# The end of a delta-rule layer as a stream of tiles, with the next layer's norm and router inside it

## The reference

```
# gated delta rule, 4 heads, keys of 64, values of 128
h = rmsnorm(layernorm(x))                      # x: the residual so far
q, k, v = l2norm(conv_silu(h @ Wq)), l2norm(conv_silu(h @ Wk)), conv_silu(h @ Wv)
o = gated_delta_rule(q, k, v, g, beta)          # scan over the 64 tokens of a sequence
o = rmsnorm(o) * o_norm_w * silu(h @ Wg)
y = x + o @ Wo                                  # here x is the block's own input (a normed x)
x = x + gelu(layernorm(y) @ W2 + b2) + y
# mixture of experts, top 1 of 8
logits = x_n @ Wr + br                          # x_n = layernorm(x) without weights
idx, gate = argmax(logits), softmax(logits)[idx]
x = x + gate * (gelu(x_n @ W1[idx] + b1[idx]) @ W2[idx] + b2[idx])
```

## Time and profile before

| | us |
|---|---|
| median of 3 runs | 843.79 |
| lowest, highest | 839.43, 844.43 |
| the profiled execution | 846.05 |
| its span | 844.3 |
| TensorE busy in the span | 684.7 (81%) |
| VectorE, ScalarE, GpSimd busy | 421.2, 328.4, 144.2 |

### The profile page before, as it was taken

One profiled execution on the slowest core, in us unless ns is written; L12 is line 12 of the kernel. 1 busy time (PEld: TensorE's weight loads), 2 busy tenths in 40 slices (PEclk: granted clock), 3 DMA queues, 4 the chain that ended last, 5 costly groups with the idle time before them and its releaser, 6 DMA issues. The chain is left out here.

```text
span 844.3 us, 18960 instructions
## 1 busy us (share of the span) xinstructions
PE 684.7 (81%) x7638; PEld 525.9 (62%) x7638; DVE 421.2 (50%) x907; ACT 328.4 (39%) x881; POOL 144.2 (17%) x213
## 2 busy tenths in 40 slices
PE   3778887789899999995787689989986764278996
PEld 2556665565456666663665546579985643178995
DVE  5436787764545445514587275836657344011111
ACT  1235444443445544442577363331224141132332
POOL 1011112201100000003334232091000211211121
PEclk9879998999999999995889699989998965598999
DMA  6920000001900000004000000000000009791110
GB/s 174 357 65 2 2 2 1 1 1 34 230 2 2 1 2 1 2 1 127 2 2 3 1 0 2 2 2 2 0 2 2 0 4 318 274 368 39 46 51 23
DMA packets 33161, 45.30 MB, mean 54 GB/s; under 512 B 7998, under 2 KB 26175, under 8 KB 32960
## 3 DMA queue, kind: packets, MB, share of 16 engines
q1 hardware_dynamic: 28672, 33.31, 12.3%
q0 software_dynamic: 2256, 7.37, 2.7%
q10 hardware_dynamic: 2160, 3.60, 1.6%
HBM read 36.91 MB, written 7.89 MB: 53 GB/s over the span
## 5 line engine op out<-in xcount | busy, mean ns | idle before, releaser
L393 ACT ACTIVATE a_pr<-a_bank,a_nms 128x160 f32<-128x160 f32 x128 | 49.1, 391 | 59.4 <-DVE a_nms L723 57.0
L859 PE MATMUL a_bank<-ident,a_pr 128*80 128x128 f32 x256 | 41.5, 289 | 25.7 <-DVE a_pt L699 23.2
L2101 ACT ACTIVATE f_hb<-f_bank,cols 128x128 f32<-128x128 f32 x96 | 35.2, 367 | 63.1 <-PE f_bank L2219 58.2
L859 PEld LDWEIGHTS a_bank<-ident,a_pr 128*80 128x80 f32 x256 | 26.1, 124 | 46.3 <-ACT a_pr L393 31.8
L2219 PE MATMUL f_bank<-f_xts,f_w 128*128 x384 | 51.6, 293 | 0.8 <-DVE f_xts L2171 0.8
L2219 PEld LDWEIGHTS f_bank<-f_xts,f_w 128*128 128x128 f32 x384 | 50.2, 208 | 1.7 <-issue 1.2
L629 DVE TENSOR_REDUCE a_negmx<-a_bank 128x2 f32<-128x320 f32 x64 | 30.4, 475 | 33.6 <-PE a_bank L851 33.6
L699 DVE COPY a_pt<-a_bank 80x512 f32<-80x512 f32 x60 | 40.9, 682 | 10.5 <-PE a_bank L859 9.8
L2229 PE MATMUL f_bank<-f_w,f_hb 128*128 128x256 f32 x192 | 44.0, 383 | 0.0
L2229 PEld LDWEIGHTS f_bank<-f_w,f_hb 128*128 128x128 f32 x192 | 36.2, 194 | 4.5
L358 POOL TENSOR_TENSOR a_spr<-a_linv,a_hm 128x128 f32<-128x128 f32 x32 | 12.1, 400 | 148.9 <-DVE a_linv L678 136.3
(11 more groups left out here) (361 smaller groups left out, 1607.2 us busy)
## 6 DMA issues: line engine op xcount, KB each, us to landing
f_w<-in_f_w SPq DMA_DIRECT2D x16, 1024.0 KB, 9.8
slots<-a_zero POOLq DMA_DIRECT2D x1, 4112.0 KB, 18.7
f_xs<-slots ACTq DMA_DIRECT2D x13, 257.0 KB, 2.7
a_ct<-in_ctxt SPq DMA_DIRECT2D x15, 160.0 KB, 5.1
rows<-in_rows SPq DMA_DIRECT2D x1, 2120.0 KB, 10.1
x<-in_x SPq DMA_DIRECT2D x2, 512.0 KB, 5.1
b_wq<-in_b_wq SPq DMA_DIRECT2D x1, 1024.0 KB, 6.2
b_wk<-in_b_wk SPq DMA_DIRECT2D x1, 1024.0 KB, 8.3
```

The lines of the kernel that those rows point to most:

```text
L393: i = act.activation(pr[:, p, j, k, :], s_bank[j][:, k * KW:(k + 1) * KW], ACT.Exp, bias=nms[:, p, j, k:k + 1], accum_out=rsum[:, p, 2 * j ...
L859: m = pe.transpose(dst[0:HK, (2 * k + a) * P:(2 * k + a + 1) * P], pr[:, p, j, k, a * HK:(a + 1) * HK], c.ident[:, :])
L2101: act.activation(hb[:, m, :], bank[m % 4][:, 0:P], ACT.Gelu, bias=c.col("f_b1", e * FC + m)).then_inc(z["act"], 1)
```

## The change

- The value buffer becomes `c.v0`, a buffer of the whole kernel; two buffers of the first stage are laid into it. `qkv` is split into `qk` and `vv = c.v0`.
- The value transposes move from behind the inversion to the place ahead of it; ScalarE copies them out of PSUM and GpSimd multiplies by `beta`. When all are transposed, SyncE loads the first expert's weights into `c.v0`.
- Behind the inversion the steps over eight tiles become one loop over `NT + 2` steps, in which each engine's queue holds the work of up to three tiles. In it, tile by tile, are the second layer norm, the GELU in two groups of four tiles, and the next stage's norm, transposes and logits in two groups.
- Every root in it is an exponential of -0.5 times a logarithm, and the table set that has both is loaded explicitly (`preload_act_table_set`).
- `stage_f` starts at the maximum of the logits. ScalarE copies the normed tiles into the rows to be scattered. Small constants come with `stage_d`'s loads. Experts 1 to 7 are loaded without the wait for the scatters.

The diff, cut to its core (`ln_vector`, `ln_scalar`, `xt_tensor` and `xt_scalar` are removed whole):

```diff
 @@ stage_d, SyncE
-            sp.wait_ge(z["weights"], 144)
+            sp.wait_ge(z["weights"], 224)
 @@ stage_e, SyncE
+            sp_.wait_ge(z["vt"], NT)
+            sp_.dma_start(vv[:, 0:2, :], c.d["f_w1"][0, :, :].rearrange("(k p) n -> p k n", p=P)).then_inc(z["expert0"], 16)
+            sp_.dma_start(vv[:, 2:4, :].rearrange("p a (m n) -> p (a m) n", n=D), c.d["f_w2"][0, :, :].rearrange("(k p) n -> p k n", p=P)
+                          ).then_inc(z["expert0"], 16)
 @@ stage_e, GpSimd, behind the gate product
+            for t in range(NT):
+                pool.wait_ge(z["vtc"], t + 1)
+                pool.tensor_tensor(bv[:, t, :, :], bv[:, t, :, :], beta[:, t, :].unsqueeze(2).to_broadcast([P, HG, VD]), ALU.mult
+                                   ).then_inc(z["bv"], 1)
 @@ stage_e, ScalarE
             act.wait_ge(z["ssq"], 1)
+            act.preload_act_table_set("natural_log_exp_and_others")
             inverse_lengths(0, bank[0][:, 0:32].rearrange("p (t h) -> p t h", h=HG))
+            for t in range(NT):
+                act.wait_ge(z["vt"], t + 1)
+                act.activation(bv[:, t, :, :].rearrange("p h n -> p (h n)"), bank[t], ACT.Copy).then_inc(z["vtc"], 1)
...
+            for t in range(NT + 2):
+                if t < NT:
+                    act.wait_ge(z["dl"], t + 1)
+                    act.activation(de[:, t, :, :].rearrange("p h n -> p (h n)"), bank[0], ACT.Copy).then_inc(z["de"], 1)
+                if t > 1:
...
+                    for k in range(KC):
+                        a = act.activation(xt2[:, u_ % 2, k, :], bank[5][:, k * P:(k + 1) * P], ACT.Identity,
+                                           scale=c.col("e_g2", k), bias=c.col("e_b2", k))
+                if 0 < t <= NT:
+                    act.wait_ge(z["ogt"], t)
+                    act.activation(de[:, t - 1, :, :].rearrange("p h n -> p (h n)"), bank[3], ACT.Copy).then_inc(z["ogs"], 1)
+                if t < NT:
+                    act.wait_ge(z["o"], t + 1)
+                    act.activation(bv[:, t, :, :].rearrange("p h n -> p (h n)"), bank[1 + t % 2], ACT.Square).then_inc(z["osq"], 1)
+                    act.wait_ge(z["oss2"], t + 1)
+                    act.activation(olog[:, head], oss2[:, head], ACT.Ln, scale=1.0 / VD, bias=eps[:, 0:1]).then_inc(z["olog"], 1)
+                    act.wait_ge(z["olog"], t + 1)
+                    act.activation(orr[:, head], olog[:, head], ACT.Exp, scale=-0.5).then_inc(z["orr"], 1)
+                if 0 < t <= NT:
...                    (logarithm and exponential of tile t - 1's variance: lrs, rs2)
+                if t in (5, 9):
...                    (GELU of four tiles)
+                    act.preload_act_table_set("natural_log_exp_and_others")
...                    (t in (6, 9): roots of the next norm; t in (7, 9): two copies of the router's transposes)
 @@ stage_e, VectorE
+            for t in range(NT + 2):
+                if t < NT:
+                    dve.wait_ge(z["osq"], t + 1)
+                    dve.reduce_sum(oss[:, head], bv[:, t, :, :], AXX).then_inc(z["oss"], 1)
+                    dve.wait_ge(z["oss"], t + 1)
+                    dve.tensor_tensor(oss2[:, head], oss[:, head], rq2[:, t, :], ALU.mult).then_inc(z["oss2"], 1)
+                if t > 1:
+                    dve.wait_ge(z["f2"], t - 1)
+                    dve.tensor_tensor(hb[:, t - 2, :], bank[6][:, 0:D], c.row("e_w2b"), ALU.add).then_inc(z["b2"], 1)
+                if t < NT:
+                    dve.wait_ge(z["orr"], t + 1)
+                    dve.tensor_tensor(ors[:, head], orr[:, head], rq[:, t, :], ALU.mult).then_inc(z["ors"], 1)
+                    dve.wait_ge(z["ors"], t + 1)
+                    for hh in range(HG):
+                        a = dve.scalar_tensor_tensor(bv[:, t, hh, :], bank[1 + t % 2][:, hh * VD:(hh + 1) * VD],
+                                                     ors[:, HG * t + hh:HG * t + hh + 1], gw[:, t, hh, :], ALU.mult, ALU.mult)
+                    a.then_inc(z["og"], 1)
+                if 0 < t <= NT:
+                    v = t - 1
+                    dve.wait_ge(z["enc"], v + 1)
+                    dve.tensor_tensor(x1[:, v, :], xl[:, v, :], bank[4][:, 0:D], ALU.add).then_inc(z["x1"], 1)
...                    (bn_stats, bn_aggr, wait for rs2, then the normed tile:)
+                    dve.tensor_scalar(xn2[:, v % 2, :], x1[:, v, :], w.mv[:, v, 0:1], rs2[:, v:v + 1], ALU.subtract, ALU.mult
+                                      ).then_inc(z["xn2"], 1)
+                if t in (5, 9):
...                    (last add to c.x and statistics of four tiles; t in (6, 9): their normed tiles, c.xn)
 @@ stage_e, TensorE, ahead of the inversion
-            pe.wait_ge(z["gate"], NT)
-            pe.wait_ge(z["lss"], 2)
+            for t in range(NT):
+                pe.wait_ge(z["gate"], t + 1)
+                if t == 0:
+                    pe.wait_ge(z["lss"], 2)
+                for hh in range(HG):
+                    a = pe.transpose(bank[t][:, hh * P:(hh + 1) * P], vv[:, hh, t * P:(t + 1) * P], c.ident[:, :])
+                a.then_inc(z["vt"], 1)
+            pe.wait_ge(z["vtc"], 4)
 @@ stage_e, TensorE, behind the inversion
+            for t in range(NT + 2):
+                if t < NT:
+                    pe.wait_ge(z["bv"], t + 1)
+                    if t:
+                        pe.wait_ge(z["de"], t)
+                    apply(bank[0], xbd, bv, t, z["dl"])
+                if t > 1:
+                    u_ = t - 2
+                    pe.wait_ge(z["xn2"], u_ + 1)
+                    if u_:
+                        pe.wait_ge(z["xt2"], u_)
+                    for k in range(KC):
+                        a = pe.transpose(bank[5][:, k * P:(k + 1) * P], xn2[:, u_ % 2, k * P:(k + 1) * P], c.ident[:, :])
+                    a.then_inc(z["xt2p"], 1)
+                if 0 < t <= NT:
+                    pe.wait_ge(z["og"], t)
...                    (four transposes of tile t - 1's output into bank 3)
+                if t < NT:
+                    pe.wait_ge(z["de"], t + 1)
...
+                    apply(bank[1 + t % 2], abd, de, t, z["o"])
+                if t > 1:
+                    pe.wait_ge(z["xt2"], u_ + 1)
...                    (second weight product of tile t - 2 into bank 6)
+                if 0 < t <= NT:
+                    pe.wait_ge(z["ogs"], t)
...                    (output projection of tile t - 1 into bank 4)
+                if t == 7:
+                    routes(0)
+            routes(1)
 @@ stage_f, SyncE
-            for e in range(E):
-                if e > 1:
+            for e in range(1, E):
+                if e > 2:
                     sp.wait_ge(s_w[e - 2], 32)
-                if e == 3:
-                    sp.wait_ge(z["scattered"], 16 * NT)
 @@ stage_f, ScalarE
-            ln_scalar(act, s, c.w)
-            xt_scalar(act, s, bank, xt)
-            act.wait_ge(z["sh"], NT)
+            for t in range(NT):
+                act.activation(xb[:, t, 0:D], c.xn[:, t, :], ACT.Copy).then_inc(z["ncopy"], 1)
+            act.wait_ge(z["sh"], 1)
 @@ stage_f, VectorE
-            for t in range(NT):
-                dve.tensor_scalar(sh[:, t, :], lg[:, t, :], mx[:, t:t + 1], None, ALU.subtract).then_inc(z["sh"], 1)
+            dve.tensor_tensor(sh[:, :, :], lg[:, :, :], mx[:, :].unsqueeze(2).to_broadcast([P, NT, E]), ALU.subtract
+                              ).then_inc(z["sh"], 1)
```

336 lines of the change are left out of this document (149 added, 187 removed).

## The result

The changed kernel takes 858.43 us (median of 4 runs, 856.49 to 859.38), against 841.84 us for the kernel before in the same session (839.43 to 844.43): ratio 1.0194, 95% interval 1.0151 to 1.0237. It is slower by some 2%, and the forecast of 855.9 us was 2.5 us short. The profiled execution has a span of 857.6 us, 13.3 more than the one before.

The account below looks back on a forecast made before the run. TensorE, busy 81%, was taken as bound, its gaps deciding. First product 627.6, stream 85.7, clock 5 and stage change 1.25 gave 719.5; the last stage's 136.9 made 856.4, less 0.5: 855.9 us, range 832 to 872.

Parts of the forecast that it names:

- the clock's term: Stream of tiles: half clock behind TensorE's pauses adds 5 us, bounds 0 and +33.
- Part 1, the hoisted transposes: Ahead of the inversion: moved value transposes and table load cost +5.0 us (3.5 to 6.5); first product at 627.6 us.
- three terms as written: Ahead of the inversion: transposes +5.2 us, table load +1.3, inversion's first product at full clock -1.5.
- Part 2, the step: Stream of tiles: one steady step is a chain of 7.8 us, against 5.4 us of TensorE work.
- The chain of hand-overs written out in the prediction: Steady step, normed tile t-2 to normed tile t-1 through TensorE, ScalarE and VectorE, each hand-over 0.04 us: 7.8 us.
- The rival that ended on the other side: Stream: engines run ahead, a step costs the busiest engine's 5.4 us, no half clock; 834 us, chance 0.16.
- the step with the GELUs: Stream: two table loads and four GELUs take 4.1 us in ScalarE's queue, of which 3.5 show.
- Part 2, the sum: Stream: logits end 85.7 us behind the first product, against 78.3 before, next norm and stage change included.
- the step without new products: Late in the stream: follows the first routing half (3.2 us ahead of tile 6's transposes), ending at 73.3 us.
- Part 3, the clock: Stream: TensorE pauses about 2.3 us each step, a quarter of the time at 1.2 GHz; +5 us.
- Part 4: Stage change and router: first maximum at 719.5 us, first scatter 8.3 us behind the stage's start, at 727.8.
- Part 5, scatters and weights: Router to expert tiles: weights beside scatters and first block load cost +7.7 us (0 to +11.5), 8.8 given back later.

Follow-up runs that it names:

- gate_3: Changed kernel with the old wait put back: weights of expert 3 and on issued only once all rows are scattered; 858.34 us, 1.0198 of the kernel before.
- deep_order: Changed kernel, same instructions and buffers, the queues of TensorE, ScalarE and VectorE reordered so each wait is for an earlier step's work; 834.36 us, 0.9894 of the kernel before.
- Move_transposes: Changed kernel with the normed tile's transposes behind the second product, and their scaled copies behind ScalarE's square; 864.58 us, 1.0256 of the kernel before.
- x1_first: Changed kernel with VectorE's residual add, statistics and their end of tile t-1 ahead of tile t's scaled products; 853.01 us, 1.0130 of the kernel before.
- fill_short: Changed kernel with four unused 256-column products in TensorE's longest pause, behind the first product of tiles 1 to 7; 856.37 us, 1.0141 of the kernel before.

## Why the prediction was right, and where its reasons were not

The mechanism was right: a step is a chain through three engines, longer than TensorE's work in it, and the weights beside the scatters are given back later. Two things in it were luck, as shown below: that the moments agree, and the size of the clock's term.

**Part 1, the hoisted transposes.** Forecast: first product at 627.6; measured 628.40. The transposes took 5.28 us (5.2 forecast) at a mean clock of 0.68, the table load stood on the path with its 1.28, and the inversion's first product took 3.95 us behind them, at full clock, where it had taken 5.50 in the kernel before at 0.69: three terms as written. That the moment agrees too is luck, since with the same code ahead of it the first product came at 622.77 in gate_3 and at 630.77 in deep_order.

```profile
556.30 1.28 ACT L1632 ACT_TABLE_LOAD   x1 [2.86 <-PE e_ps L1849]
...
558.03 5.28 PE L1925 MATMUL e_ps<-ident,v 128*128 128x128 f32 x32 [1.75 <-ACT e_lss L1599]
563.24 3.95 PE L1934 MATMUL e_ps<-e_xinv,e_cv 64*64 64x64 f32 x128
```

The last of these rows in the kernel before:

```profile
556.71 5.50 PE L1913 MATMUL e_ps<-e_xinv,e_cv 64*64 64x64 f32 x128 [0.42 <-issue]
```

**Part 2, the step.** The chain of hand-overs written out in the prediction is the ring of the trace, entry for entry, at 7.37 us in place of 7.76. Most of the 0.4 is the price of a transpose: 0.163 us, taken from a group that ran partly at half clock, so 0.98 for six, where the ring shows 0.72 from 667.86 to 668.58. What failed is the sentence behind it, that the step is long "because the transposes of tile t-2 stand ahead of the second product of tile t in TensorE's queue". That is one link of the ring. Move_transposes shows that to move it alone gains nothing, as ScalarE's copy behind the norm's roots holds the second product at the same moment, and that the step gets 0.27 us longer, as the projection then waits behind the scaled copies. The ring exists because all three queues take up work of the same step in a fixed order: x1_first shortens it from VectorE's side, and deep_order, which loosens all three, removes it. The rival that ended on the other side asked for the right thing, TensorE's work as the bound. Its price for a plain step is borne out by deep_order, where the step fell from 7.37 to 5.03 us, so 2.3 against the 2.4 of the rival. Seven times that is 16 of the 25.2 us that deep_order took out between first product and first scatter. In the rest are the step with the GELUs (11.73 us, where no step of deep_order is longer than 5.75) and the clock; no run splits it. The condition, three queues in another order, isn't met by the change.

**Part 2, the sum.** The step with the GELUs cost 12.44 us between two normed tiles (11.2 forecast), and the end behind the last normed tile 14.0 (12.4). The first normed tile came at 16.4 us in place of 14.0, with TensorE's clock at 0.61 and 0.52 in the windows from 628 to 640. In all 90.6 us from the first product to the end of the logits; the prediction had 85.7, and 5 for the clock, 90.7. That the two agree is luck. Against the 85.7 us, the first normed tile is 2.4 us late, the step with the GELUs 1.2 longer, the step without new products 0.8 longer (10.0 against 9.2) and the end 1.6, together 6.0; the five plain steps are 1.1 shorter (37.8 against 38.9). The difference, 4.9, is what the prediction gave to the clock.

**Part 3, the clock.** The mean clock fell as forecast, to 0.81 in the stretch. The size, +5, stands only in part: 2.1 us of it are shown by fill_short for the steps, and in the tail the same instructions took 3.8 us more at 0.63 than at 0.75. The Trainium skill ("TensorE: Matmul & The Clock Gate", A second HAM failure mode) describes this swing between half and full clock for a kernel with short pauses between groups of products. The traces agree that the clock falls, and that work in the pauses brings it back to 1.00; but the stretch to the logits stayed at 90.9 us (90.6 unfilled), since the tail, unfilled, lost 2.4 us where the steps had gained 2.1.

The table loads cost 1.28 us each and no more. The Trainium skill ("ScalarE: Activation LUTs", What ACT_TABLE_LOAD costs) adds a drain of about 1.38 us; the trace disagrees for a load between GELUs and exponentials too, in rows of ScalarE's timeline that follow one another without a gap (the exponential ahead of them ends at 674.67):

```profile
674.69 1.28 ACT L1674 ACT_TABLE_LOAD   x1
675.99 1.33 ACT L1674 ACTIVATE e_xinv<-e_xinv 128x256 f32<-128x256 f32 x4
677.34 1.28 ACT L1675 ACT_TABLE_LOAD   x1
678.63 0.60 ACT L1645 ACTIVATE e_gate<-e_ps 128x512 f32<-128x512 f32 x1
```

**Part 4.** The first scatter was forecast for 727.8 and came at 728.04. The stage's first maximum came 0.8 us late (720.30 against 719.5), and from there to the scatter it took 7.74 us, not 8.3. The terms that the prediction gives add up to 8.5 (8.6 before, less 0.9, plus 0.8), so the 8.3 doesn't follow from them.

**Part 5, scatters and weights.** Forecast: 24.7 us from first scatter to first tile, measured 24.4. The price of +7.7 for the weights beside the scatters was 7.4; it splits into 5.9 for the scatters (5.2 forecast) and 1.5 for the first block load (2.5). Given back: 8.8 forecast, 7.5 measured; the step that was off is that only one wait of 2.6 us would stay, where three stayed, 3.7 us together. The two terms nearly cancel, which gate_3 confirms.

**The rest of the total.** From the first tile to the end 105.2 us against 103.9 forecast, the span 857.6 against 856.4. The other 1.3 us of the 2.5 lie in the step from span to median: 0.5 less was forecast, and it was 0.8 more.

## What to carry to other kernels

When a stage of steps over all tiles is turned into a stream of tiles, write down for each engine the order in which its queue takes up the tiles, and follow one round of waits until it closes: its length is the step, however idle every engine is. If it is longer than the busiest engine's work, let each engine take up results of an earlier step, on all queues at once; moving the work of one tile in one queue made the full-clock step 0.3 us longer in one place and 0.2 shorter in another, and all three queues together made it 2.3 shorter. A wait that orders two transfers that share the DMA queues can be nearly neutral both ways, as it was here in both kernels, so look for what it gives back before counting what it costs.

## What the runs showed of the hardware that I had not expected

Eight scatters with no expert weights beside them reach the block load's issue 11.9 us after the first, with 4 MB of weights issued 7.8 us ahead of them 12.5, and with a stream of weights that outlasts them 17.1 to 18.0 us: what is still under way when the last scatters land costs 5 to 6 us, what was issued that early 0.6.

GpSimd's prices did not carry over. The eight multiplies of the betas took 8.06 us where eight of the same shape in the kernel before took 12.01, and a multiply of 128x32 elements behind them, of 0.26 us before, took 2.39 us while VectorE ran a multiply of 128x2048 (2.88 us in place of 2.28):

```profile
560.51 8.06 POOL L1551 TENSOR_TENSOR e_qk<-e_qk,e_rden 128x512 f32<-128x512 f32 x8
568.50 2.39 POOL L1554 TENSOR_TENSOR e_rq<-e_rss 128x32 f32<-128x32 f32 x1
...
567.91 2.88 DVE L1735 TENSOR_TENSOR e_cv<-e_dts,e_mt 128x2048 f32<-128x2048 f32 x1
```

Neither was on the path here, and no run of this study isolates the cause.
